# Six output-weight tiles split before the first scores of a latent attention, and four of their product triples left in its tail

## The chip, the cores and the metric

One core of one Trainium2 chip runs the whole program in one launch. The metric is the device time in microseconds (us). TensorE is written PE, VectorE DVE, ScalarE ACT, GpSimd POOL; SP is the engine that issues the DMAs.

## The reference

Four residual blocks over a `(4, 512, 1024)` tensor, each with a layer norm ahead of it. All is float32 at the interface; the kernel carries each matrix operand as a high and a low float16 half and multiplies with three matmuls (high by high, high by low, low by high).

```python
x = x + _L0_attn_ref(_layernorm(x))                 # small attention over the batch axis
x = x + _L0_ffn_ref(_layernorm(x), ...)             # linear + top-2 routed LoRA
x = x + _L1_attn_ref(_layernorm(x), ...)            # 32 heads, causal, 512 tokens x 4 batches
x = x + _L1_ffn_ref(_layernorm(x), ...)             # linear + routed LoRA
# the third one:
q = rmsnorm(x @ wq_a.T) @ wq_b.T ; kv = rmsnorm(ckv) @ wkv_b.T ; rope on q_pe, k_pe
attn = softmax(causal(q_full . k_full * scale))
out = (attn @ v).reshape(B, S, 32 * 128) @ wo.T
```

## The kernel before

The program is a row of blocks, each with five instruction streams (PE, ACT, DVE, POOL, SP) and a barrier of all engines between two blocks: `first` (A), `lora_layer0` (F0), `projections` (C), `attention` (D), `out_projection` (E), `lora_layer1` (F1). An engine works its stream strictly in the written order and waits on semaphores.

**The output weights.** A folds the value half of `wkv_b` into `wo`; the product, 16 tiles of 128x1024 float32 called kt 0 to 15, lies in device memory (`mwd`). Class `OutWeights` takes them in: `sp_load` fetches tile kt into one of three raw buffers (512 KB each; it waits until tile kt - 3 has been split), `act_high` writes its high half (ACT, L479) and `dve_low` its low half (DVE, L483). EARLY = 6 tiles have their halves in `ow_mh`, `ow_ml`, placed before the attention; the other ten live in E. `pe_product(j, kt)` multiplies the attention output of token tile j, transposed by a DMA into `ow_ot`, with tile kt: six matmuls of 512 columns. One product triple is a kt for the token tiles j = 0, 1, 2: 18 matmuls.

**The attention, D.** 128 units u = 0 to 127, one head of one batch for 512 queries each, in a software pipeline that runs u from FIRST = -7 to 134. In round u:
- PE: `scores(u)` (12 matmuls of 512, 384, 256 and 128 columns in three parts, L1657 to L1659, and the causal mask L1666), `values(u-5)` (30 matmuls, L1681 to L1683), `query(u+7)` (6 matmuls of 512), `turn_q(u+2)` (four transposes, L1640); from round 129 on also a product triple.
- ACT: the third part of the exponentials of u-1, `high_p(u-1)` (L1722, the high half of the probabilities), `high_o` (L1741), the first two parts of `exps(u)` (L1714), `nope(u+7)` (L1729), `high_q(u+2)` (L1734), and in the rounds 20, 36, 52, 68, 84, 100 of the table SPLIT one `act_high`.
- DVE: `least` (L1769, the row minima), `bias` (L1778), `rotate(u+6)` (L1799 to L1802), `normalize(u-5)` (L1784, L1788), `low_q(u+2)` (L1807), and in the rounds of SPLIT one `dve_low`.
- POOL: `add_q(u+6)` (L1840), `low_p(u-1)` (L1834), `low_o(u-6)` (L1846).
- SP: `turn_p(u-2)` (L1862, the transpose of the probabilities by DMA, which `values` and, three units on, `high_p` wait for); every 16 rounds `load_w` (L1866, 512 KB of query weights, rounds -6, 10, 26, ... 90); every four rounds `store_o` (L1872, 512 KB of outputs to `od`); three `sp_load` in round 8 (L474), one each in rounds 24, 40, 56, 72, 88, 104; the first pieces of the `ow_ot` transposes (L488, `sp_turn_piece`) in rounds 124, 125, 126, and the second ones in 130 to 132.

Two waits tie the stages: `query(u)` waits for the rotation of unit u-2 (`s_qm`), and part n of the scores waits for the exponentials of part n-4, whose bank it takes:

```python
w.wait_ge(s_qm, u - 1)             # query(u), PE
w.wait_ge(s_exp, n - 3)            # scores, part n, PE
w.wait_ge(s_tl, u + 1)             # scores(u), PE: low_q(u) on DVE is done
w.wait_ge(s_pt[(u - 3) % 4], ...)  # high_p(u), ACT: the transpose of unit u-3 has landed
w.wait_ge(s_ol, u - 1)             # normalize(u), DVE: low_o(u-2) on POOL is done
```

In E the products go on from kt = EARLY, ACT and DVE split the tiles 6 to 15, whose first three raw tiles were loaded in D, and SP fetches the rest and the last `ow_ot` pieces.

Of the kernel before, what the change touches and what calls it, by code (L numbers as in the profile page):

```python
# [17 lines left out]
NT = 16  # L18
# [165 lines left out]
def layers(nc, a, out):  # L184
    root = ExitStack()
    with root:
# [31 lines left out]
        with ExitStack() as right:  # L218
            feed.place(right, "N", "right", 0, (3, 3, 4))
            g["wa"] = SmallWeights(nc, right, a["wa"])  # L220
            lora_layer0(**g)
            g["qT"] = [m("qTh", [128, 2, 2048], H16), m("qTl", [128, 2, 2048], H16)]
# [4 lines left out]
        with ExitStack() as late:  # L227
            ow.raw = [late.enter_context(nc.sbuf_tensor(f"rm{i}", [128, 1024], F, side="right")) for i in range(3)]
            with ExitStack() as outs, ExitStack() as last:
                ow.place(outs)  # L230
                ow.ob = [outs.enter_context(nc.psum_tensor(f"so{i}", [128, 512], F)) for i in range(6)]
                attention(**g)
                mid.close()
                feed.place(last, "N1", "left", 2 * NT, (1, 2, 3))
                lw.place(lambda name, shape, dt=F: last.enter_context(nc.sbuf_tensor(f"F1_{name}", shape, dt)), 1, a,
                         [r[:, 0:784] for r in ow.raw])
                out_projection(**g)
                outs.close()
                lora_layer1(**g)
# [200 lines left out]
class OutWeights:  # L440
# [4 lines left out]

    def __init__(self, nc, root, mwd, od, ms):
# [5 lines left out]

    def place(self, ctx):
# [3 lines left out]
        self.early = [sb(f"m{x}", [128, self.EARLY, 1024]) for x in "hl"]  # L457
# [951 lines left out]
def projections(nc, a, wbs, s_wb, s_xd, cst, half, ident, xb, qT, kT, v, wb0, norm, feed, wa, **_):  # L1409
# [143 lines left out]
    def sp(e):  # L1553
        w = Waits(e)
        e.dma_start(wb0[:, :, :, :], wbs[0]).then_inc(s_wb, 16)
        for t in range(3, NT):
            feed.sp_turn(e, w, NT + t)
        w.wait_ge(s_xd, 16 * NT)
# [10 lines left out]
def attention(nc, wbs, od, s_wb, s_ot, cst, ident, xb, qT, kT, v, wb0, qw, ow, **_):  # L1569
# [35 lines left out]
    SPLIT = [20 + 16 * i for i in range(ow.EARLY)]  # L1605
# [12 lines left out]
    def pe(e):  # L1618
# [67 lines left out]
        for u in range(FIRST, LAST):  # L1686
# [8 lines left out]
            if NU < u <= NU + ow.EARLY:  # L1695
# [7 lines left out]
    def act(e):  # L1703
# [39 lines left out]
        for u in range(FIRST, LAST):  # L1743
            if there(u - 1):
# [11 lines left out]
            if u in SPLIT:  # L1756
                ow.act_high(e, w, SPLIT.index(u))

    def dve(e):
# [49 lines left out]
        for u in range(FIRST, LAST):  # L1809
            if there(u):  # L1810
# [13 lines left out]
            if u in SPLIT:  # L1824
                ow.dve_low(e, w, SPLIT.index(u))
# [30 lines left out]
    def sp(e):  # L1856
# [18 lines left out]
        for u in range(FIRST, LAST):  # L1875
# [6 lines left out]
            if u == SPLIT[0] - 12:  # L1882
                for kt in range(3):
                    ow.sp_load(e, w, kt)
# [512 lines left out]
```

## Time and profile before

| | us |
|---|---|
| median of 3 runs | 1730.37 |
| lowest, highest | 1725.38, 1730.89 |
| the profiled execution | 1732.51 |
| its span | 1730.7 |
| PE busy (share of the span) | 1597.3 (92%) |
| DVE busy | 1029.0 (59%) |
| ACT busy | 873.0 (50%) |
| POOL busy | 816.6 (47%) |
| mean granted TensorE clock | 0.963 |

The profile is of one execution; its own time (1732.51) is its span and 1.8 us around it. Busy shares are means over stages with different limits, so the attention (from about 553 to 1188 us of the span) has to be read by itself. An engine's idle time before an instruction stands in square brackets in the timeline, with what ended it. Matmuls are pipelined: the duration of one overlaps the next, and the distance between two starts is what it costs.

### The profile page before, as it was taken

To read this page: it belongs to the slowest core of one execution; us is meant where nothing else is said; L and a number is where in the kernel's file an instruction comes from. 1 tells how busy PE (TensorE), PEld (TensorE's weight loads), DVE (VectorE), ACT (ScalarE), POOL (GpSimd) and SP (SyncE) were. 2 spreads that over 40 slices of the span, in tenths; PEclk is the share of its full clock that TensorE was granted. 3 is DMA by queue.
4 is the path that set the end of the run, shared out by engine and by line. 5 is a ranking of instruction groups with operands and counts; after the bars stand their busy time and mean duration, and the time that the engine had idled before them with its cause. 6 is when DMAs were issued, how large, how long until landed. Compare 5 with 4: busy or idle time off the path is not lost. (4 is left out here: it accounts for less than half of the span.)

```text
span 1730.7 us, 32183 instructions
## 1 busy us (share of the span) xinstructions
PE 1597.3 (92%) x12482; PEld 980.2 (57%) x12482; DVE 1029.0 (59%) x2766; ACT 873.0 (50%) x1670; POOL 816.6 (47%) x702
## 2 busy tenths in 40 slices
PE   5899579999787999999999999979999999999998
PEld 5566345555443667666767667744444444465554
DVE  5599456776486888888888888852111001154433
ACT  4676322222264899999999999962110000021110
POOL 2222224444474678888888888860010000044440
PEclk7799789999898999999999999989999999999999
DMA  9574333454543599998989999996775413033231
GB/s 320 168 261 173 110 110 86 134 146 122 122 86 62 99 210 172 197 183 169 212 169 194 191 188 187 173 195 173 211 185 113 98 31 79 12 102 86 74 86 74
DMA packets 559608, 249.32 MB, mean 144 GB/s; under 512 B 502240, under 2 KB 535008, under 8 KB 559072
## 3 DMA queue, kind: packets, MB, share of 16 engines
q1 hardware_dynamic: 559456, 247.26, 62.7%
q8 instruction: 99, 1.62, 0.4%
q14 instruction: 53, 0.43, 0.1%
HBM read 73.15 MB, written 48.23 MB: 70 GB/s over the span
## 5 line engine op out<-in xcount | busy, mean ns | idle before, releaser
L1834 POOL TENSOR_TENSOR xb<-xb 128x1280 f16<-128x1280 f32 x128 | 335.4, 2620 | 7.6 <-ACT xb L1722 7.6
L1714 ACT ACTIVATE xb<-so,D_sv,qw_c 128x512 f32<-128x512 f32 (+3 forms) x512 | 288.7, 621 | 8.2 <-DVE D_sv L1778 8.1
L1769 DVE TENSOR_REDUCE so<-so 128x1 f32<-128x512 f32 (+3 forms) x512 | 227.7, 491 | 7.8 <-PE so L1666 7.3
L1722 ACT ACTIVATE xb<-xb 128x1280 f16<-128x1280 f32 x128 | 162.6, 1271 | 15.2 <-DMA xb<-xb 11.3
L1657 PE MATMUL so<-kTh,D_QTh 128*128 128x512 f16 (+3 forms) x512 | 153.6, 300 | 15.8 <-ACT xb L1714 15.8
L92 POOL TENSOR_SCALAR mv<-mv 128x1 f32<-128x1 f32 x64 | 27.6, 431 | 285.9 <-DVE mv L87 284.8
L1958 DVE SCALAR_TENSOR_TENSOR xb<-so,ms_c,xb 128x512 f32<-128x512 f32 x32 | 22.5, 746 | 228.2 <-PE so L50 228.2
L1658 PE MATMUL so<-kTl,D_QTh 128*128 128x512 f16 (+3 forms) x512 | 153.2, 299 | 0.0
L1659 PE MATMUL so<-kTh,D_QTl 128*128 128x512 f16 (+3 forms) x512 | 146.6, 299 | 0.0
L168 POOL TENSOR_TENSOR N_hl<-N_h,N_hl 128x1024 f16<-128x1024 f32 x48 | 103.6, 2158 | 88.3 <-ACT N_hl L163 88.2
L1840 POOL TENSOR_TENSOR D_qs<-D_qs,D_t 128x256 f32<-128x256 f32 x128 | 92.9, 726 | 90.6 <-DVE D_t L1802 90.6
L1681 PE MATMUL D_t<-vh,xb 128*128 128x65 f16 x1280 | 132.2, 195 | 3.3 <-DVE D_on L1788 3.3
L1682 PE MATMUL D_t<-vl,xb 128*128 128x65 f16 x1280 | 132.3, 193 | 0.0
L1683 PE MATMUL D_t<-vh,xb 128*128 128x65 f16 x1280 | 131.7, 194 | 0.0
L1807 DVE TENSOR_TENSOR D_QTl<-D_t,D_QTh 128x512 f16<-128x512 f32 x128 | 88.6, 692 | 63.8 <-ACT D_QTh L1734 63.8
L48 PE MATMUL so<-E_mh,ow_ot 128*128 128x512 f16 x320 | 121.9, 381 | 2.9 <-DVE E_ml L483 2.9
L50 PE MATMUL so<-E_mh,ow_ot 128*128 128x512 f16 x320 | 122.0, 381 | 0.0
L49 PE MATMUL so<-E_ml,ow_ot 128*128 128x512 f16 x320 | 121.9, 381 | 0.0
L1681 PEld LDWEIGHTS D_t<-vh,xb 128*128 128x128 f16 x1280 | 119.6, 98 | 3.8 <-issue 1.7
L1682 PEld LDWEIGHTS D_t<-vl,xb 128*128 128x128 f16 x1280 | 119.3, 99 | 0.4
L1683 PEld LDWEIGHTS D_t<-vh,xb 128*128 128x128 f16 x1280 | 119.5, 97 | 0.0
L163 ACT ACTIVATE N_hl<-N_h 128x1024 f16<-128x1024 f32 x48 | 50.4, 1050 | 112.0 <-DVE N_h L105 111.6
(248 smaller groups left out, 4245.6 us busy)
## 6 DMA issues: line engine op xcount, KB each, us to landing
A_wo<-in_wo SPq DMA_DIRECT2D x16, 1024.0 KB, 6.1
od<-D_os SPq DMA_DIRECT2D x32, 512.0 KB, 4.4
mwd<-A_mst SPq DMA_DIRECT2D x32, 256.0 KB, 2.4
xd<-xb SPq DMA_DIRECT2D x16, 512.0 KB, 4.1
rm<-mwd SPq DMA_DIRECT2D x16, 512.0 KB, 5.0
xb<-xd SPq DMA_DIRECT2D x16, 512.0 KB, 5.8
out_x<-xb SPq DMA_DIRECT2D x16, 512.0 KB, 3.3
xb<-in_x SPq DMA_DIRECT2D x6, 1024.0 KB, 19.7
```

The source lines that it names most:

```text
L48: e.matmul(out, a[0], b[0], start=start, stop=False, **kw)
L50: return e.matmul(out, a[1], b[0], start=False, stop=stop, **kw)
L1657: e.matmul(ps, qh, kT[0][:, k0:k0 + M], start=i > 0, stop=False)
L1658: e.matmul(ps, qh, kT[1][:, k0:k0 + M], start=False, stop=False)
L1659: e.matmul(ps, ql, kT[0][:, k0:k0 + M], start=False, stop=False)
L1681: e.matmul(o, pt[:, c, :], v[0][:, t, 0:65], start=j == 0, stop=False)
L1682: e.matmul(o, pt[:, c, :], v[1][:, t, 0:65], start=False, stop=False)
L1683: m = e.matmul(o, pt[:, 10 + c, :], v[0][:, t, 0:65], start=False, stop=j == i)
L1714: m = e.activation(p[:, AT[i]:AT[i] + N], Sb[n % 4][:, c:c + N], ACT.Exp, scale=qw.col(qw.NEG, g), bias=s[:, 7 - i:8 - i])
L1722: e.activation(P2[u % 3][:, 0:1280], P[u % 3][:, :], ACT.Copy).then_inc(s_ph, 1)
L1769: m = e.tensor_reduce(minima(u, i), Sb[n % 4][:, c:c + N], AX.X, ALU.min)
L1834: e.tensor_tensor(P2[u % 3][:, 1280:2560], P[u % 3][:, :], P2[u % 3][:, 0:1280], ALU.subtract).then_inc(s_pl, 1)
```

## The change

The six tiles are no longer split in the rounds 20 to 100 but in the rounds -7 (kt 0, 1, 2), -2 (kt 3) and -1 (kt 4, 5), at the head of the round on ACT and DVE. Their raw buffers and halves are placed ahead of the projections, whose SP stream loads tiles 0 to 2 at its end; tiles 3 to 5 are loaded in round -7, tiles 6 to 8 together in round 64. PE does the triples of kt 0 to 3 in D (rounds 129 to 132) and those of kt 4 and 5 at the head of E. The first `ow_ot` pieces are issued in rounds 123 to 125. The raw buffers are named `ow_raw` now.

```diff
     EARLY = 6
+    AHEAD = 4
+    def place_weights(self, ctx):
+        def sb(name, shape, dt):
+            return ctx.enter_context(self.nc.sbuf_tensor(f"ow_{name}", shape, dt))
+        self.raw = [sb(f"raw{i}", [128, 1024], F) for i in range(3)]
+        self.early = [sb(f"m{x}", [128, self.EARLY, 1024], H16) for x in "hl"]
...
 # projections, sp
         for t in range(3, NT):
             feed.sp_turn(e, w, NT + t)
+        for kt in range(3):
+            ow.sp_load(e, w, kt)
         w.wait_ge(s_xd, 16 * NT)
...
 # attention
-    SPLIT = [20 + 16 * i for i in range(ow.EARLY)]
+    SPLIT = [FIRST, FIRST, FIRST, -2, -1, -1]
...
 # pe
-            if NU < u <= NU + ow.EARLY:
+            if NU < u <= NU + ow.AHEAD:
...
 # act (and dve with ow.dve_low)
         for u in range(FIRST, LAST):
+            for kt in range(ow.EARLY):
+                if SPLIT[kt] == u:
+                    ow.act_high(e, w, kt)
...
-            if u in SPLIT:
-                ow.act_high(e, w, SPLIT.index(u))
...
 # sp
-            if u == SPLIT[0] - 12:
-                for kt in range(3):
+            if u == FIRST:
+                for kt in range(3, ow.EARLY):
                     ow.sp_load(e, w, kt)
-            if u - 4 in SPLIT:
-                ow.sp_load(e, w, SPLIT.index(u - 4) + 3)
-            if u == NU - 4:
+            if u == NU // 2:
+                for kt in range(ow.EARLY, ow.EARLY + 3):
+                    ow.sp_load(e, w, kt)
+            if u == NU - 5:
                 w.wait_ge(s_ot[0], 16 * 15)
-            if NU - 4 <= u < NU - 4 + ow.G:
-                ow.sp_turn_piece(e, u - NU + 4, 0)
+            if NU - 5 <= u < NU - 5 + ow.G:
+                ow.sp_turn_piece(e, u - NU + 5, 0)
...
 # out_projection, pe
-        for kt in range(EARLY, 12):
+        for kt in range(ow.AHEAD, 12):
```

The start of D on DVE, as the change has it (L1808 to L1811 is a rotation, L1816 a `low_q`, L1778 the first minima; before, they were L1799 to L1802, L1807 and L1769):

```order
L489 SCALAR_TENSOR_TENSOR ow_ml<-ow_raw,ms_c,ow_mh 128x1024 x3
L1808 TENSOR_TENSOR D_qs<-so,cst 128x4x64
L1810 TENSOR_TENSOR D_t<-so,cst 128x4x32
L1811 TENSOR_TENSOR D_t<-so,cst 128x4x32
...
L489 SCALAR_TENSOR_TENSOR ow_ml<-ow_raw,ms_c,ow_mh 128x1024
L1808 TENSOR_TENSOR D_qs<-so,cst 128x4x64
L1810 TENSOR_TENSOR D_t<-so,cst 128x4x32
L1811 TENSOR_TENSOR D_t<-so,cst 128x4x32
L1816 TENSOR_TENSOR D_QTl<-D_t,D_QTh 128x512
L489 SCALAR_TENSOR_TENSOR ow_ml<-ow_raw,ms_c,ow_mh 128x1024 x2
```

Three low halves stand ahead of the first rotation, one ahead of the fifth, and two between the first and the second `low_q`; before there was none here. ACT has its six `act_high` in the same rounds.

The end of D on SP, before (L1862 is `turn_p`, L488 a piece of `ow_ot`, L1872 a store):

```order
L1862 DMA_TRANSPOSE xb<-xb 128x20x128 x2
L488 DMA_TRANSPOSE ow_ot<-od 128x8x128
L1862 DMA_TRANSPOSE xb<-xb 128x20x128
L488 DMA_TRANSPOSE ow_ot<-od 128x8x128
L1862 DMA_TRANSPOSE xb<-xb 128x20x128
L1872 DMA od<-D_os 128x4x512
L488 DMA_TRANSPOSE ow_ot<-od 128x8x128
L1862 DMA_TRANSPOSE xb<-xb 128x20x128 x3
```

and now (L1872 is `turn_p`, L494 a piece, L1882 a store):

```order
L1872 DMA_TRANSPOSE xb<-xb 128x20x128
L494 DMA_TRANSPOSE ow_ot<-od 128x8x128
L1872 DMA_TRANSPOSE xb<-xb 128x20x128
L494 DMA_TRANSPOSE ow_ot<-od 128x8x128
L1872 DMA_TRANSPOSE xb<-xb 128x20x128
L494 DMA_TRANSPOSE ow_ot<-od 128x8x128
L1872 DMA_TRANSPOSE xb<-xb 128x20x128
L1882 DMA od<-D_os 128x4x512
L1872 DMA_TRANSPOSE xb<-xb 128x20x128 x3
```

Each of the three pieces now goes out one `turn_p` earlier: they stand ahead of the transposes of units 122, 123 and 124.

## Rows read from the trace of the kernel before

**Rows 1.** Windows of the attention's middle: busy us (count) of PE, PEld, DVE, ACT, POOL, clock, DMA share, GB/s
```profile
625.00:1126.00 501.00, 492.67 (x6105) 352.13 (x6104) 436.12 (x1309) 484.73 (x877) 433.84 (x327) 1.00 0.99 185
```

**Rows 2.** Timeline of PE and ACT, one unit apart: start us, us, engine, line, tiles
```profile
755.93 0.38 PE L1657 MATMUL so<-kTh,D_QTh 128*128 128x512 f16 x1
760.43 0.38 PE L1657 MATMUL so<-kTh,D_QTh 128*128 128x512 f16 x1
...
758.30 1.27 ACT L1722 ACTIVATE xb<-xb 128x1280 f16<-128x1280 f32 x1
762.71 1.27 ACT L1722 ACTIVATE xb<-xb 128x1280 f16<-128x1280 f32 x1
```

**Rows 3.** Waits from 625 to 1126 us: total us, times, longest
```profile
PE so L1657 <- ACT xb L1714: 8.3, 8, 1.4
ACT xb L1722 <- DMA xb<-xb: 7.1, 7, 2.3
```

**Rows 4.** Timeline of the first split unit, on ACT, DVE and PE
```profile
662.59 1.16 ACT L479 ACTIVATE ow_mh<-rm,ms_c 128x1024 f16<-128x1024 f32 x1
663.78 1.99 DVE L483 SCALAR_TENSOR_TENSOR ow_ml<-rm,ms_c,ow_mh 128x1024 f16<-128x1024 f32 x1 [0.35 <-ACT ow_mh L479]
666.65 0.38 PE L1659 MATMUL so<-kTh,D_QTl 128*128 128x512 f16 x1
667.97 0.34 PE L1657 MATMUL so<-kTh,D_QTh 128*128 128x384 f16 x1 [0.94 <-ACT xb L1714]
```

**Rows 5.** Waits of ACT for a transpose of the probabilities, and PE after the first
```profile
617.86 1.27 ACT L1722 ACTIVATE xb<-xb 128x1280 f16<-128x1280 f32 x1 [3.15 <-DMA xb<-xb]
703.46 1.27 ACT L1722 ACTIVATE xb<-xb 128x1280 f16<-128x1280 f32 x1 [1.93 <-DMA xb<-xb]
778.21 1.27 ACT L1722 ACTIVATE xb<-xb 128x1280 f16<-128x1280 f32 x1 [2.32 <-DMA xb<-xb]
...
620.15 0.34 PE L1657 MATMUL so<-kTh,D_QTh 128*128 128x384 f16 x1 [1.96 <-ACT xb L1714]
```

**Rows 6.** Windows after the stalls at 620, 1160 and 1188 us, columns as in rows 1
```profile
620.00:625.00 5.00, 4.85 (x48) 3.46 (x49) 3.48 (x11) 4.97 (x10) 3.17 (x4) 0.66 0.93 256
1160.00:1165.00 5.00, 5.00 (x16) 1.85 (x15) 0.00 (x0) 0.00 (x0) 0.15 (x1) 0.61 1.18 232
1188.00:1195.00 7.00, 4.17 (x12) 1.64 (x13) 3.68 (x3) 3.23 (x3) 0.00 (x0) 0.76 0.86 133
```

**Rows 7.** Line 483 by form: ns min/median/max, first and last start
```profile
L483 DVE SCALAR_TENSOR_TENSOR E_ml<-rm,ms_c,E_mh x10: 1277/1284/1286, 1189.4 to 1211.8; 128x1024 f16<-128x1024 f32 x10
L483 DVE SCALAR_TENSOR_TENSOR ow_ml<-rm,ms_c,ow_mh x6: 1840/1853/1987, 663.8 to 1033.6; 128x1024 f16<-128x1024 f32 x6
```

**Rows 8.** Timeline of the start of the attention, on PE, DVE and ACT
```profile
553.00 0.58 PE L48 MATMUL so<-wb,qTh 128*128 128x512 f16 x1 [1.69 <-PEq L1560]
...
556.17 0.42 DVE L1799 TENSOR_TENSOR D_qs<-so,cst 128x256 f32<-128x256 f32 x1 [3.49 <-ACT D_qs L1729]
567.39 1.16 DVE L1769 TENSOR_REDUCE so<-so 128x1 f32<-128x512 f32 x2 [0.42 <-PE so L1666]
...
568.85 1.34 ACT L1714 ACTIVATE xb<-so,D_sv,qw_c 128x512 f32<-128x512 f32 x2 [2.60 <-DVE D_sv L1778]
```

**Rows 9.** Timeline of the end of the attention, on SP, DVE and PE
```profile
1148.83 3.63 SPq L1862 DMA_TRANSPOSE xb<-xb  x1
...
1153.13 1.50 SPq L488 DMA_TRANSPOSE ow_ot<-od  x1
...
1153.90 0.42 DVE L1788 TENSOR_TENSOR D_on<-D_t,D_sv 128x256 f32<-128x256 f32 x1 [0.81 <-POOL D_os L1846]
...
1159.66 0.58 PE L48 MATMUL so<-ow_mh,ow_ot 128*128 128x512 f16 x1 [3.38 <-DMA ow_ot<-od]
```

**Rows 10.** PE on the two sides of the barrier between attention and output projection
```profile
1187.57 0.38 PE L50 MATMUL so<-ow_mh,ow_ot 128*128 128x512 f16 x1
1190.83 0.38 PE L48 MATMUL so<-E_mh,ow_ot 128*128 128x512 f16 x1 [2.89 <-DVE E_ml L483]
```

More of the change, by code:

```diff
@@ L221, in layers @@
             lora_layer0(**g)
+            ow.place_weights(root)
             g["qT"] = [m("qTh", [128, 2, 2048], H16), m("qTl", [128, 2, 2048], H16)]
@@ L226, in layers @@
             projections(**g)
[L227 to L239, printed above, removed]
+        with ExitStack() as outs, ExitStack() as last:
+            ow.place(outs)
+            ow.ob = [outs.enter_context(nc.psum_tensor(f"so{i}", [128, 512], F)) for i in range(6)]
+            attention(**g)
+            mid.close()
+            feed.place(last, "N1", "left", 2 * NT, (1, 2, 3))
+            lw.place(lambda name, shape, dt=F: last.enter_context(nc.sbuf_tensor(f"F1_{name}", shape, dt)), 1, a,
+                     [r[:, 0:784] for r in ow.raw])
+            out_projection(**g)
+            outs.close()
+            lora_layer1(**g)
 class Scope:
@@ L456, in place @@
         self.OT = [sb(f"ot{i}", [128, 8, 2, 2, 128]) for i in range(self.G)]
-        self.early = [sb(f"m{x}", [128, self.EARLY, 1024]) for x in "hl"]
     def pe_product(self, e, w, j, kt):
@@ L1406, in lora_layer0, with projections @@
     ph.ctx.close()
-def projections(nc, a, wbs, s_wb, s_xd, cst, half, ident, xb, qT, kT, v, wb0, norm, feed, wa, **_):
+def projections(nc, a, wbs, s_wb, s_xd, cst, half, ident, xb, qT, kT, v, wb0, norm, feed, wa, ow, **_):
     ph = Scope(nc, "C")
@@ L1809, in dve @@
         for u in range(FIRST, LAST):
+            for kt in range(ow.EARLY):
+                if SPLIT[kt] == u:
+                    ow.dve_low(e, w, kt)
             if there(u):
@@ L1823, in dve @@
                 low_q(u + 2)
-            if u in SPLIT:
-                ow.dve_low(e, w, SPLIT.index(u))
     def pool(e):
```

## The prediction

> **What bounds the kernel now.** First the windows of the attention's middle [rows 1]: PE is busy 492.67 of 501 us at full clock and ACT 484.73, so both are nearly full, and a busy share alone does not say which one sets the pace. So next two consecutive units [rows 2]: PE starts its scores 4.50 us apart (755.93 to 760.43) with no idle time noted, ACT starts `high_p` 4.41 us apart (758.30 to 762.71). ACT's round is the shorter by 0.09 us: PE sets the pace as long as nothing interrupts, and ACT wins back 0.09 us a unit after an interruption, until it has caught up. The cost of an interruption is therefore what it leaves on PE. The waits of that stretch [rows 3] say how often: PE waited for ACT's exponentials 8 times, 8.3 us. Six of the eight are the units with a split, two lie right behind ACT's longest waits for a transpose of the probabilities. The two places behind the middle where PE stands are the first product triple and the barrier [rows 9, 10]. The last stages, from 1195 us on, are PE at full work, and nothing there changes but when they start.
>
> By 0.3% either way I mean 5.2 us of the 1730.37, about what a measurement of this kernel can tell from no change. I sum against the profiled execution's own 1732.5 us, which is 2.1 us above the median of the runs.
>
> **1. The six splits leave the middle: -6.6 us.** In the first one [rows 4] ACT works 1.16 us on the high half and DVE 1.99 on the low one, starting one after the other; `high_p` then comes 2 us late over two units, and of this 1.10 us reach PE: the next part of the scores starts 1.32 us after the one before instead of 0.22. So about 0.9 us of slack is there ahead of an interruption and the rest is PE's. The five later ones repeat it within 0.01 us. 6 x 1.10 = 6.6. What covered them is PE's own round, and that is what remains: 4.50 us a unit. Bounds: 0.94 each as the idle time noted (5.6) to 1.16 each, all of ACT's piece (7.0).
>
> **2. Loads against transposes: -1.1 us.** The transposes of the probabilities take the DMA queue nearly all the time (DMA share 0.99, rows 1). The three loads of round 8 went out in one go ahead of one; ACT waited 3.15 us, PE 1.96 by the idle time noted, 2.12 by starts [rows 5], and then ran from 620 to 625 us at a granted clock of 0.66, which is 1.2 GHz for two thirds of it: 5 x 0.34 = 1.7 us more [rows 6]. The single loads of rounds 24 and 40 came two rounds before a `load_w`, and ACT waited 1.93 and 2.32 us [rows 5]; behind it PE lost 8.3 - 6 x 0.94 = 2.7 us by the waits [rows 3], 3.0 by starts. In all 2.1 + 1.7 + 3.0 = 6.8. After the change no tile is loaded in these rounds, but `load_w` stays with its store beside it, and from this trace I can't separate the two. I leave 1.0 us at round 10 and 0.5 each at 26 and 42, two fifths of the old ones. The three loads now meet at round 64. The nearest row is that of round 8: ACT waits 3.15, the full slack of 0.9 is there, PE loses 2.2, and the clock may fall as it did, 1.7 more. That is 5.9 against 6.8, so -1 us. Bounds: nothing at all is left (-6.8), or everything stays and the loads of round 64 come on top with a fall of the clock (+3.9).
>
> The Trainium skill, "DMA: Bandwidth & Descriptors", section Queues, rings and completion order, says that each DMA engine consumes its descriptors in ring order, and this speaks against bundling loads on the queue of the transposes: what is issued first is in the way whatever it is for. The row at 617.86 us agrees.
>
> **3. The six splits at the start: +4.7 us.** This is the price. The new duration of a low half is bounded by two rows [rows 7]: 1.28 us in the output projection, where POOL is idle, 1.85 in the attention's middle, where POOL works all the time. In rounds -7 to -1 POOL has only the short additions, so I take 1.28. By the Trainium skill, "SBUF — State Buffer", section Who interferes with whom, a DVE instruction with two SBUF inputs contends with a POOL instruction that reads SBUF; it would put these six at the uncontended duration too. No run here shows them at this place yet.
> Step by step from 553.0 [rows 8]: ACT starts the three high halves at once (their raw tiles were loaded about 10 us earlier), DVE starts its first at 554.2 and ends the third at 554.2 + 3 x 1.28 = 558.0. The first rotation starts there instead of at 556.17, +1.8. Queries go in pairs behind rotations (`query(u)` waits for the rotation of u-2), so PE stands about 1.4 us ahead of `query(2)` and runs 1.2 us late until `query(5)` ends at 564.2. The fourth high half waits behind `nope(4)` and ends at 564.4; its low half puts the fifth rotation and the first `low_q` to 565.7 and 566.5. Two low halves (2.6 us) then stand before the sixth rotation and the second `low_q`, which ends at 571.0. The first minima follow, at 571.0 instead of 567.39, and the first exponentials at 572.5 instead of 568.85: +3.65. From there the first units go at ACT's pace, as before, so all of it arrives. To this I add 1.0 for the clock: PE now stands still three times for 1.4 to 2 us, and a stand of 2.1 us was followed by a fall [rows 5, 6]. Bounds: 3.0, if the raw tiles' waits and the pairs overlap better; 3.65 + 6 x 0.57 = 7.1 with the low halves at 1.85, and 8 with two falls of the clock. The loads at the end of the projections stand behind all transposes of that stage, and the tiles 3 to 5 in round -7 are ahead of nothing but a `load_w` that is needed 16 units later: 0.
>
> **4. The first piece transposes go one unit earlier: -3.0 us.** PE waited 3.38 us for the third piece before the first triple (to 1159.66) [rows 9]. Issued ahead of the transpose of unit 124 instead of behind it, the piece goes out some 4.4 us earlier (1153.13 to about 1148.7) and lands before PE asks. But each piece takes the SP queue 1.3 to 1.5 us in front of a transpose that `high_p` waits for: the last units slip by 1.4 at the most, `values(124)` with them (its turn hangs on `normalize`, which hangs on POOL, which hangs on `high_p`). So the triple starts at about 1156.7 in the old times. Bounds: 0 to 3.6. PE is at half clock there in both (0.61 from 1160 to 1165 us) [rows 6], so no more comes of it.
>
> **5. Two triples cross the barrier: -4.2 us.** Each is 18 matmuls of 512 columns at some 0.22 us from start to start [rows 4], 3.9 us, in both kernels: moved, not saved. But E began with a wait: PE's last start in D is 1187.57, its first in E 1190.83 [rows 10], since the raw tile 6 could only be split by ACT (1.15) and DVE (1.28) behind the barrier. Now 7.8 us of products with halves that are long ready stand there, and the splits of tiles 6, 7 and 8 run beside them. Of the 3.26 us about 0.75 remain for the barrier itself (between C and D, ACT, DVE and PE are at work 0.3 us after the last engine's end), -2.5. The clock fell behind this wait as well: 7 x 0.24 = 1.7 us [rows 6], which goes with it. Bounds: -1.5 to -4.3. The new pieces of `ow_ot` that E asks for at kt 8 were in time by less than a microsecond; now PE comes to kt 8 3.9 us later after the barrier, so they are late nowhere.
>
> **Sum.** -6.6 - 1.1 + 4.7 - 3.0 - 4.2 = -10.2 us: 1722.3 of the profiled 1732.5. Against the median that is **1720**.
>
> **Rivals.**
> *The start and the loads eat more.* The low halves take 1.85 us at the start, or the clock falls twice (+8 instead of +4.7), and the `load_w` stalls stay as they are (+1 instead of -1.1). For it: the start is a chain with no slack (DVE idles there only behind ACT and PE). Against it: POOL idles. -10.2 + 3.3 + 2.1 = -4.8: 1725.5.
> *The loads hide.* The pair of a load and a `load_w` did harm, not either alone: the single load of round 104, which had no `load_w` behind it, made nobody wait, and of the 7 waits counted [rows 3] six came behind a pair and one, 0.7 us, behind the single load of round 24. And the pairs of rounds 72 and 88 cost PE nothing. Then the old 6.8 go and round 64 costs little, with the start at 3.7: -10.2 - 4.7 - 1.0 = -16: 1714.5.
> *The DMA becomes the bound (slower).* The transposes fill the queue (0.99), and the PE gaps of the splits were time in which they caught up. If the queue and not PE's 4.50 us holds the middle, the six gaps come back as waits of ACT for transposes, the pieces at the end gain nothing (they only push transposes), and round 64 adds 2.7. It decides when a transpose lands later than `high_p` three units on can bear, some 2.9 us beyond what an undisturbed one takes. Then +2.7 + 4.7 - 4.2 = +3.2: 1733.6. Against it: between the loads ACT never waits for a transpose [rows 3], even in stretches of 16 units.
> *The change doesn't do what it says.* The order of the instructions shows the splits where they are meant to be; only part 4 could be without effect, and 0 is in its bounds.
>
> **How the numbers follow.** 1720 with its own range of 1717 to 1724: 0.57. The start eats more, around 1725.5: 0.19. The loads hide, around 1714.5: 0.17. The DMA bound, around 1733.6: 0.07. The range 1714 to 1726 takes in the first, more than half of the second and most of the third. Faster by over 0.3% is below 1725.2: all of the first and third and a third of the second, 0.80. Within 0.3%: the rest of the second and most of the fourth, 0.17. Slower: 0.03.
>
> **What would show it.** In the middle no idle time of PE at rounds 20 to 100, and 4.50 us a unit throughout; the wait of ACT for a transpose near round 66, about 3 us, and smaller ones after rounds 10, 26, 42. The first minima 3.5 to 5 us later after the barrier than now (14.4 us), and low halves of 1.28 us. The first triple without a wait for `ow_ot`, and the first E matmul within 1 us of D's last at clock 1.00. The prediction is wrong if the start costs over 8 us, or if PE's gaps come back in the middle with ACT waiting for transposes.

## The result, and the profile after

Over six runs each the changed kernel takes 1712.78 us (1711.59 to 1715.57), the one before 1727.49 (1725.38 to 1730.89; the three runs known at the prediction lay high, their median was 1730.37). The ratio is 0.9914 with a 95% interval of 0.99 to 0.9929, so the change takes off 14.7 us (12.3 to 17.3), where 10.2 were forecast. The sign was right. The time lies 1.2 us below the range's low end, 1714.

| | before, us | after, us | |
|---|---|---|---|
| the profiled execution, its span | 1732.5, 1730.7 | 1713.0, 1711.2 | -19.5 in the span |
| `first` (A), same code | 188.6 | 183.2 | -5.4 |
| layer 0's second block, projections, layer 1's second block | 585.9 | 586.8 | +0.9 |
| D: first query to the first `high_p` | 18.79 | 22.26 | +3.5 |
| D: from there to `low_q(120)` | 542.90 | 531.13 | -11.8 |
| D: from there to the first triple | 44.98 | 44.51 | -0.5 |
| D: from there to the last `values` | 16.43 | 16.02 | -0.4 |
| last `values` to F1's first matmul | 333.09 | 327.29 | -5.8 |

From D's first query to F1 that is -15.0, which agrees with the times. The 5.4 us of `first` are no effect of the change: its code is the same, and over all seventeen profiles of this study it lasts 180.9 to 188.6 us, in the kernels with the old attention as in those with the new. The two executions profiled lay nearly at the two ends. Every comparison below is therefore made inside D and E, or by medians of many runs on one chip.

Windows of the profile after; columns as in rows 1:

```profile
625.00:1108.00 483.00, 480.95 (x5984) 345.79 (x5983) 421.00 (x1280) 472.67 (x854) 420.17 (x320) 1.00 0.98 185
870.00:875.00 5.00, 3.37 (x49) 2.40 (x50) 2.04 (x5) 4.97 (x10) 3.25 (x2) 1.00 1.13 261
1146.00:1151.00 5.00, 5.00 (x25) 2.16 (x23) 0.61 (x2) 1.07 (x4) 4.46 (x4) 0.63 1.09 216
1166.00:1173.00 7.00, 6.55 (x32) 2.80 (x30) 3.67 (x3) 3.23 (x3) 0.00 (x0) 1.00 0.77 173
1356.00:1366.00 10.00, 10.00 (x54) 6.17 (x53) 1.96 (x5) 2.57 (x3) 1.01 (x1) 0.83 0.51 107
```

The same two stretches of the kernel before (the last one lies 20 us later there):

```profile
625.00:1108.00 483.00, 474.67 (x5879) 338.90 (x5878) 420.24 (x1261) 466.85 (x845) 418.12 (x315) 1.00 0.99 186
1376.00:1386.00 10.00, 10.00 (x46) 5.98 (x45) 1.97 (x5) 2.62 (x3) 1.01 (x1) 0.66 0.50 107
```

In the middle PE stands still for 2.05 us of 483 and no longer for 8.3. Nearly all of what is left is one place. Waits of the middle after, from 590 to 1108 us (total us, times, longest):

```profile
ACT xb L1730 <- DMA xb<-xb: 7.1, 5, 3.0
PE so L1665 <- ACT xb L1722: 2.1, 2, 1.8
```

The same for the kernel before, from 590 to 1126 us:

```profile
ACT xb L1722 <- DMA xb<-xb: 10.3, 8, 3.1
PE so L1657 <- ACT xb L1714: 10.3, 9, 2.0
```

ACT still waits five times for a transpose, 7.1 us in all, but PE notices only two of the five. The longest is the one that the three loads of round 64 cause, in the timeline of SP, ACT and PE:

```profile
857.57 1.60 SPq L480 DMA_DIRECT2D ow_raw<-mwd  x3
859.27 10.35 SPq L1872 DMA_TRANSPOSE xb<-xb  x2
...
869.33 1.27 ACT L1730 ACTIVATE xb<-xb 128x1280 f16<-128x1280 f32 x1 [2.97 <-DMA xb<-xb]
...
871.63 0.34 PE L1665 MATMUL so<-kTh,D_QTh 128*128 128x384 f16 x1 [1.80 <-ACT xb L1722]
```

It is the stall of round 8 over again ([rows 5]: 3.15 and 1.96), moved to round 64. In this profile the clock did not fall behind it: 1.00 from 870 to 875 us, against 0.66 in [rows 6]. In another profile of the same kernel (changed_fourth, below) it did, and as far as before:

```profile
875.00:880.00 5.00, 4.89 (x49) 3.69 (x50) 3.40 (x10) 4.97 (x10) 2.93 (x3) 0.66 1.10 246
```

Where `act_high` used to stand, nothing interrupts PE, and the single `load_w` of rounds 10, 26, 42 leave it 0.42 us in all, all of it behind round 26. (Over the twelve profiles with a `load_w` alone in round 26 and no split in the middle, this place costs 0 to 0.83 us.)

The start of D, on ACT, DVE and PE:

```profile
548.46 3.23 ACT L485 ACTIVATE ow_mh<-ow_raw,ms_c 128x1024 f16<-128x1024 f32 x3 [1.02 <-PEq L1568]
549.63 3.68 DVE L489 SCALAR_TENSOR_TENSOR ow_ml<-ow_raw,ms_c,ow_mh 128x1024 f16<-128x1024 f32 x3 [1.48 <-ACT ow_mh L485]
553.23 0.42 DVE L1808 TENSOR_TENSOR D_qs<-so,cst 128x256 f32<-128x256 f32 x1
...
562.54 2.57 DVE L489 SCALAR_TENSOR_TENSOR ow_ml<-ow_raw,ms_c,ow_mh 128x1024 f16<-128x1024 f32 x2
...
566.36 1.15 DVE L1778 TENSOR_REDUCE so<-so 128x1 f32<-128x512 f32 x2
...
562.17 0.38 PE L48 MATMUL so<-wb,qTh 128*128 128x512 f16 x1 [1.92 <-DVE D_t L1811]
```

D's first query is at 548.48 here (553.00 in [rows 8]). The first low half starts 1.15 us behind it, the first minima 17.9 us behind it, where they used to be 14.4 behind. The low halves, by the view of line 489 (ns min/median/max):

```profile
L489 DVE SCALAR_TENSOR_TENSOR ow_ml<-ow_raw,ms_c,ow_mh x6: 1272/1284/1378, 549.6 to 563.8; 128x1024 f16<-128x1024 f32 x6
```

They take 1.28 us and not the 1.85 of the middle [rows 7], with POOL nearly idle. The Trainium skill, "SBUF — State Buffer", section Who interferes with whom, says that a DVE instruction with two SBUF inputs contends with a POOL instruction that reads SBUF; the trace agrees. PE stood still twice, for 1.06 and 1.92 us, and the clock was 1.00 behind both.

The end of D, on SP and PE:

```profile
1125.82 1.30 SPq L494 DMA_TRANSPOSE ow_ot<-od  x1
1127.20 3.67 SPq L1872 DMA_TRANSPOSE xb<-xb  x1
1130.92 1.90 SPq L494 DMA_TRANSPOSE ow_ot<-od  x1
1132.91 3.32 SPq L1872 DMA_TRANSPOSE xb<-xb  x1
1136.28 1.30 SPq L494 DMA_TRANSPOSE ow_ot<-od  x1
1137.68 3.51 SPq L1872 DMA_TRANSPOSE xb<-xb  x1
...
1136.50 0.34 PE L1665 MATMUL so<-kTh,D_QTh 128*128 128x384 f16 x1 [1.61 <-ACT xb L1722]
1144.73 0.24 PE L1689 MATMUL D_t<-vh,xb 128*128 128x65 f16 x1 [3.13 <-DMA xb<-xb]
...
1146.37 0.62 PE L48 MATMUL so<-ow_mh,ow_ot 128*128 128x512 f16 x1
```

The first triple no longer waits for its piece (3.38 us in [rows 9]). In its place the products with V wait 3.13 us for a transpose of the probabilities, which stands behind the pieces on SP. In this pair of profiles the wait changed its name and hardly its size; the other profiles, below, show that this is not the rule.

The barrier, on PE; the last matmul of D and the first of E:

```profile
1166.09 0.38 PE L50 MATMUL so<-ow_mh,ow_ot 128*128 128x512 f16 x1
1166.92 0.38 PE L48 MATMUL so<-ow_mh,ow_ot 128*128 128x512 f16 x1 [0.45 <-PEq L1906]
```

0.83 us from start to start, against 3.26 in [rows 10], and the clock stays at 1.00 behind it (0.76 in [rows 6]).

### The profile page after: what moved, and what is told of

Read it like the earlier page. It is cut to its first block and busy times, and to the rows that moved or that the text cites. A ratio compares the mean times of both kernels' runs of the same rounds, so it can differ in the third digit from the quotient of the medians.

```text
span 1711.2 us, 32182 instructions
## 1 busy us (share of the span) xinstructions
PE 1585.0 (93%) x12482; PEld 974.3 (57%) x12482; DVE 1028.6 (60%) x2766; ACT 875.8 (51%) x1670; POOL 810.7 (47%) x702
## 5 line engine op out<-in xcount | busy, mean ns | idle before, releaser
L1778 DVE TENSOR_REDUCE so<-so 128x1 f32<-128x512 f32 (+3 forms) x512 | 228.1, 492 | 19.3 <-PE so L1674 18.6
L1816 DVE TENSOR_TENSOR D_QTl<-D_t,D_QTh 128x512 f16<-128x512 f32 x128 | 88.5, 692 | 48.7 <-ACT D_QTh L1742 48.7
```

The source lines that it names most:

```text
L1778: m = e.tensor_reduce(minima(u, i), Sb[n % 4][:, c:c + N], AX.X, ALU.min)
```

## Experiments

Ratios are to the kernel before, run on the same chip in turn with the experiment, with their 95% interval. "Middle" is the fifth row of the table above; the kernel before has 542.90 us there, the changed one 531.13. "Gap" is a distance between two PE starts, less what it is in an undisturbed unit.

### Only part 5, and only part 4

**ahead_only** is the kernel before, with two triples taken across the barrier:

```diff
-            if NU < u <= NU + ow.EARLY:
+            if NU < u <= NU + 4:
...
-        for kt in range(EARLY, 12):
+        for kt in range(4, 12):
```

> The kernel before with only part 5 of the change: PE does the triples of kt 0 to 3 in the attention's tail and those of kt 4 and 5 at the head of the output projection. The prediction's theory: -4.2 us, the wait of 3.3 us at the barrier down to 0.75 and the fall of the clock behind it gone. What the changed kernel's trace suggests: up to -5.8, since the stretch behind the last values became 5.8 us shorter there; if that surplus of 1.6 is not of the barrier but of where the clock falls at the small column sums in the output projection, this kernel shows it or not by chance, and the gap at the barrier alone gives 4 to 4.3. A rival, that the splits in the middle hold the time and the tail is covered: 0.

Measured: 0.9973 (0.9959 to 0.9987) of 1725.3 us, that is -4.7 us (-7.1 to -2.2). From the last `values` to F1 its trace takes 327.30 us, just as the changed kernel, instead of 333.09. PE across the barrier:

```profile
1178.37 0.38 PE L48 MATMUL so<-ow_mh,ow_ot 128*128 128x512 f16 x1 [0.45 <-PEq L1895]
```

Of the 5.8 us, 2.4 are the gap at the barrier (3.05 to 0.61), 1.7 the slow clock behind it, and 1.7 a term that the sum did not have: 190 us later PE does sums over single columns, and the clock falls behind them, to 0.66 over ten microseconds before, to 0.83 here as in the changed kernel (windows above), 10 x 0.17 = 1.7 us less. Whether an edit does this is open; it comes up again below. Nor is the slow clock behind the old barrier there every time: loads_moved and pieces_only (both below) have the same start-to-start distance of 3.27 us at it, and the clock falls behind it in loads_moved and stays at 1.00 in pieces_only. The gap is the sure part of the gain.

**pieces_only** is the kernel before with its pieces issued one unit earlier (`NU - 4` made `NU - 5` in its three places).

> The kernel before with only part 4: the first three pieces of ow_ot go out in rounds 123 to 125 instead of 124 to 126. The prediction's theory: -3.0 us (0 to -3.6), since PE waited 3.4 us for the third piece. The rival, from the changed kernel's trace: the pieces push the transposes of units 122 to 124 by 1.3 us each and these add up, so that values(124) comes about as late as the third piece did: -0.5 us, with no wait for ow_ot but longer waits of ACT for transposes (over 1 us three times) before it.

Measured: 0.9989 (0.9973 to 1.0004), -1.9 us (-4.7 to +0.7): no difference that is sure. From `low_q(120)` to the last `values` its trace takes 58.1 us, against 61.4 before. The first triple comes 1.8 us earlier (43.2 us behind `low_q(120)` for 45.0), and between it and the last `values` the slow clock took 0.6 us here and 2.1 there.

### The pieces back, in the changed kernel

**pieces_back** undoes part 4 alone:

```diff
-            if u == NU - 5:
+            if u == NU - 4:
                 w.wait_ge(s_ot[0], 16 * 15)
-            if NU - 5 <= u < NU - 5 + ow.G:
-                ow.sp_turn_piece(e, u - NU + 5, 0)
+            if NU - 4 <= u < NU - 4 + ow.G:
+                ow.sp_turn_piece(e, u - NU + 4, 0)
```

> The changed kernel with its pieces back in rounds 124 to 126. The prediction's theory: 3.0 us slower than the changed kernel. The rival, that the earlier pieces pay for themselves with pushed transposes: within 1 us of it, with the wait for the third piece (3 us) back before the first triple and the waits of ACT for transposes gone.

Measured: 0.9942 (0.9922 to 0.9962), with the changed kernel not on the same chip. So both were run side by side twice more.

> The changed kernel once more, beside the next one on one chip: about 14 us below before. In its trace the time from the 121st low half of the queries to the first triple is 43 to 44.5 us, as in the two profiles of it so far.

> The changed kernel with its pieces back in rounds 124 to 126, beside the changed kernel on the same chip, since the two were compared over different chips. The prediction's theory: 3.0 us slower. What the profiles so far suggest (44.7 us to the first triple against 43.1 to 44.5): no more than 1.5 us slower, as pushed transposes pay for the earlier pieces.

The changed kernel took 1712.13 us, the one with the pieces back 1715.02: 2.9 us. Once more on another chip:

> The changed kernel, beside the next one on one chip, for the price of the earlier pieces: 0.991 of the time before, as three times already.

> The changed kernel with its pieces back in rounds 124 to 126. So far 0.9942 and 0.9936 of the time before against 0.9914, 0.9911 and 0.9910 of the changed kernel, some 4 us, while the profiles showed no difference from the last units to the output projection (387.3 to 387.9 us here, 384.9 to 387.8 there). The prediction's theory: 3.0 us slower once more, so that the profiles were the slower executions of the changed kernel. The rival: under 1 us.

1713.81 and 1714.84: 1.0 us, with ratios whose intervals overlap (0.9908 to 0.9939, and 0.9918 to 0.9947), as they do in the first pair (0.9884 to 0.9937, and 0.9913 to 0.9958). With pieces_only this makes three comparisons by whole runs, all with the earlier pieces ahead, by 1.0 to 2.9 us; these runs settle the price of part 4 no closer.

The traces scatter as much. Counted from `low_q(120)`, those of the first pair reach the first triple after 44.2 us (changed) and 43.6 (pieces back), and the last `values` after 60.4 and 60.1; those of the second pair after 43.5 and 44.9, and after 58.6 and 62.1. One pair shows no gain, the other 1.4 and 3.5 us. Over the fifteen profiles with the pieces in these rounds, the six with rounds 124 to 126 reach the first triple after 43.6 to 45.5 us (mean 44.6) and the last `values` after 60.1 to 62.7 (61.2); the nine with 123 to 125 after 42.7 to 44.7 (43.7) and 57.6 to 61.2 (59.2). By the means the edit gains 0.9 and 2.0 us, with ranges that overlap.

Two things stand against each other there. The wait for a piece before the first triple, 0.9 to 4.1 us in the six, is gone in all nine. But a piece ahead of the transposes of units 122, 123 and 124 makes `high_p` of the following units late (in the first pair those of units 124 to 127 come 24.0, 29.3, 32.9 and 39.1 us behind the scores of unit 120, with the pieces back 23.2, 27.3, 31.0 and 37.5), and the `values` behind them. The wait of the `values` for a transpose, 3.13 us in the profile above, is not of the edit alone: waits of 1.9 to 3.1 us stand there in four of the nine and in three of the six.

### The loads, taken apart

**loads_spread** is the changed kernel with tiles 6, 7 and 8 loaded one at a time, far from any `load_w`:

```diff
-            if u == NU // 2:
-                for kt in range(ow.EARLY, ow.EARLY + 3):
-                    ow.sp_load(e, w, kt)
+            if u in (52, 68, 84):
+                ow.sp_load(e, w, ow.EARLY + (u - 52) // 16)
```

> The changed kernel with the three loads of round 64 apart, one each in rounds 52, 68 and 84, six rounds ahead of a load of query weights. If three loads in one go are what costs (ACT waits 3 us, PE loses 2.0 in the changed kernel's trace): -2 us against the changed kernel, no wait of ACT over 1 us between 840 and 900 us. If any load of 512 KB costs PE its share wherever it stands: no change, three smaller stalls.

Measured: 0.9898 (0.988 to 0.9915), -17.6 us. The middle takes 528.93 us and its one gap is 0.35 us. Its window and waits, as for the changed kernel (the waits from 590 to 1105 us):

```profile
625.00:1108.00 483.00, 482.82 (x6020) 347.76 (x6018) 424.18 (x1286) 476.54 (x857) 421.86 (x322) 1.00 0.98 186
```

```profile
ACT xb L1730 <- DMA xb<-xb: 3.2, 4, 1.4
PE so L1665 <- ACT xb L1722: 0.2, 1, 0.2
```

So the burst of round 64 costs 2 us (1.75 to 2.12 in its seven profiles), and a tile load by itself nothing. That a pair would have cost more does not follow from this run: its loads also stand late, where the pairs of the kernel before cost PE nothing either. loads_moved and loads_paired ask about that.

**loads_moved** asks the same of the kernel before: all six splits stay in the middle, and only the loads of tiles 0 to 5 and 6 to 8 move away from round 8 and from the `load_w`.

```diff
-            if u == SPLIT[0] - 12:
+            if u == FIRST:
                 for kt in range(3):
                     ow.sp_load(e, w, kt)
-            if u - 4 in SPLIT:
-                ow.sp_load(e, w, SPLIT.index(u - 4) + 3)
+            if u - 13 in SPLIT:
+                ow.sp_load(e, w, SPLIT.index(u - 13) + 3)
```

> The kernel before with its splits where they were, but its tile loads away from the loads of query weights: three in round -7, one each in rounds 33, 49, 65, 81, 97, 113, seven rounds behind a load of query weights. If it is the pair that does harm (a tile load two rounds ahead of a load of query weights with its store): PE's gaps behind waits for transposes (1.8, 1.5, 1.3 us in three profiles) shrink to under 0.5 each and the kernel is 4 to 5 us faster than before. If the load of query weights does it by itself, as the prediction assumed for two fifths of it: only the 1.8 us of round 8 go and 0.5 each of the others, -2 to -3 us.

Measured: 0.9969 (0.9951 to 0.9987), -5.3 us (-8.4 to -2.2), without a split or a triple touched. Its waits from 590 to 1115 us:

```profile
ACT xb L1722 <- DMA xb<-xb: 5.5, 6, 1.8
PE so L1657 <- ACT xb L1714: 6.4, 7, 0.9
```

PE's gaps are the six of the splits, 1.10 us each as before, and one of 0.91, behind the `load_w` of round 42, which now stands by itself. In the kernel before they were 2.12 behind the three loads of round 8, 1.61 behind the pair of rounds 24 and 26, and 1.42 behind that of rounds 40 and 42. The tile loads of rounds 33 and 49, nearly as early and alone, cost nothing. The middle is 537.45 us, against 542.90.

**loads_paired** is the changed kernel with tiles 6, 7 and 8 loaded where the old kernel had its singles, two rounds ahead of a `load_w` (`if u in (24, 40, 56)` in loads_spread).

> The changed kernel with its three loads of round 64 apart, one each in rounds 24, 40, 56, two rounds ahead of a load of query weights, as the tile loads stood in the kernel before. The run with rounds 52, 68, 84 lost 0.4 us of PE in the whole middle. If the pair does the harm by itself: ACT waits some 2 us for a transpose at two or three of these places and PE loses 0.5 to 1.5 us behind each, 2 to 4 us in all over that run. If it took the splits of the middle to make the pairs hurt (they used up ACT's slack): PE loses under 1 us.

Measured: 0.9917 (0.9892 to 0.9942), -14.3 us. The middle takes 530.65 us, with gaps of 0.92 and 1.07 behind the first two pairs and none behind the third; waits from 590 to 1105 us:

```profile
ACT xb L1730 <- DMA xb<-xb: 5.5, 4, 2.1
PE so L1665 <- ACT xb L1722: 1.7, 2, 0.9
```

What a place costs PE, over all profiles (us; n is their number):

| | `load_w` alone | with a tile load two rounds ahead |
|---|---|---|
| round 26, no split in the middle | 0 to 0.83, n = 12 | 0.92, n = 1 |
| round 42, no split in the middle | 0, n = 12 | 1.07, n = 1 |
| round 26, splits in the middle | 0, n = 1 | 1.43 to 1.61, n = 3 |
| round 42, splits in the middle | 0.91, n = 1 | 1.25 to 1.42, n = 3 |
| rounds 58, 74, 90, with or without splits | 0 | 0, once 0.46 |

A tile load alone costs nothing anywhere. The pair costs more than the `load_w` alone at rounds 26 and 42, with the splits and without them, by 0.1 to 1.6 us; at the later rounds it costs next to nothing. The runs don't show why the place matters. In times, loads_paired (0.9892 to 0.9942) and loads_spread (0.988 to 0.9915) are not surely apart.

### Other places for the splits

The changed kernel was run again beside these.

> The changed kernel itself, as the reference for the other three of this call on the same chip: 0.9914 of the time before (0.990 to 0.993) was measured. Every theory gives that again. Its stage times in the trace say how much of a difference between two profiles is chance: the small attention of layer 0 (the first 180 us) differed by 5 us between the two profiles though its code is the same.

0.9911 (0.9884 to 0.9939), 1709.59 us where the kernel before took 1723.6.

**three_in_tail** splits tiles 3 to 5 in D's last rounds, where ACT and DVE have little to do, and loads 6 to 8 behind the last piece instead of in round 64:

```diff
-    SPLIT = [FIRST, FIRST, FIRST, -2, -1, -1]
+    SPLIT = [FIRST, FIRST, FIRST, 129, 130, 131]
...
-            if u == NU // 2:
-                for kt in range(ow.EARLY, ow.EARLY + 3):
-                    ow.sp_load(e, w, kt)
...
                 ow.sp_turn_piece(e, u - NU - 2, 1)
+                if u == NU + 4:
+                    for kt in range(ow.EARLY, ow.EARLY + 3):
+                        ow.sp_load(e, w, kt)
```

> The changed kernel with the splits of tiles 3, 4, 5 in rounds 129 to 131, where ACT and DVE stand idle, and tiles 6 to 8 loaded in round 132 instead of together in round 64. If the start costs by its chain of DVE work: three of six low halves go, the first exponentials come 2.0 to 2.5 us earlier (19 to 20.3 us to the first high half of the probabilities instead of 22.3), and the 2 us that PE loses at round 64 go too: -4 us against the changed kernel. If the start's price is the wait for the first split (ACT, then DVE) and not the number of splits: only the 2 us of round 64. Should the tiles 6 to 8 arrive late, PE waits at the third triple of the output projection.

Measured: 0.9893 (0.9866 to 0.9919), 1707.52 us, 2.1 below the changed kernel, where 4 were expected. The start is 20.01 us instead of 22.27, and the middle 528.73 instead of 530.40. The tail takes some of this back in the trace: 61.2 us from `low_q(120)` to the last `values`, the longest of the nine profiles with the pieces in rounds 123 to 125, with the clock at half for 13.7 us. Whether the splits of the last rounds do this is open. And the middle shows what it is without any tile's load or split:

```profile
600.00:1100.00 500.00, 500.00 (x6217) 360.02 (x6216) 439.60 (x1333) 493.52 (x890) 436.69 (x334) 1.00 0.97 183
```

PE is busy for 500 of 500 us, with the transposes at a DMA share of 0.97. From the scores of unit 6 to those of unit 120 it takes 513.6 us, and 114 units of 4.50 are 513: the middle is PE's, and there is nothing left in it to win but PE's own work.

**splits_in_C** is loads_spread with all six splits in the projections, at every second token tile from 4 to 14, and their loads between the feeds there:

```diff
+    AT_T = [4, 6, 8, 10, 12, 14]
...
+            if t in AT_T:
+                ow.act_high(e, w, AT_T.index(t))
...
+            if t in AT_T:
+                ow.dve_low(e, w, AT_T.index(t))
```

> The kernel with one load each in rounds 52, 68, 84, and all six splits inside the projections, one every second tile on ACT and DVE, where ACT waits 2 us in each tile for POOL; nothing is split in the attention. If that stage is held by its chain over POOL and the slack of ACT and DVE takes the splits: the projections stay at 93 us, the attention's start goes back to 18.8 us, and the kernel is 5.5 us faster than the changed one. If the splits delay the chain: up to 1.2 us each, 7 us in the projections, and the gain is gone.

Measured: 0.991 (0.9884 to 0.9935), 1709.82 us. D starts 3.3 us faster (19.00 us), and the projections take 96.5 us instead of 93.6 (92.3 to 94.9 in all other profiles): what the start of D paid is paid there. Beside loads_spread nothing is won.

### The pieces where their data is ready

**pieces_mid** takes the six piece transposes of `ow_ot` out of the tail. The first three read what the units up to 19 have stored, the other three what those up to 51 have, so they can go out in the middle of D:

```diff
-            if u == NU - 5:
-                w.wait_ge(s_ot[0], 16 * 15)
-            if NU - 5 <= u < NU - 5 + ow.G:
-                ow.sp_turn_piece(e, u - NU + 5, 0)
-            if NU + 2 <= u < NU + 2 + ow.G:
-                ow.sp_turn_piece(e, u - NU - 2, 1)
+            if u in (48, 64, 80):
+                w.wait_ge(s_ot[0], 16 * 3)
+                ow.sp_turn_piece(e, (u - 48) // 16, 0)
+            if u in (96, 104, 112):
+                w.wait_ge(s_ot[0], 16 * 7)
+                ow.sp_turn_piece(e, (u - 96) // 8, 1)
```

and the three loads of round 64 stand in round 68.

> The changed kernel with all six early pieces taken out of the attention's last rounds: the pieces of kt 0 to 3 in rounds 48, 64, 80, those of kt 4 to 7 in rounds 96, 104, 112 (the head groups that they transpose are stored by rounds 26 and 58), and the tile loads of round 64 in round 68. If it is pieces against transposes on the SP queue that holds the tail: ACT's waits for transposes in the last five units shrink from 1 to 1.5 us each to under 0.5, the first triple comes without a wait, 3 to 5 us less from the last units to the first triple, and the middle loses under 1 us. If the last values hang on DVE, ACT and POOL alone: 1 us or less.

Measured: 0.9876 (0.985 to 0.9902), 1706.79 us, where the changed kernel took 1712.13 on the same chip: -5.3, for the pieces and the moved loads together. SP in the tail:

```profile
1121.89 14.90 SPq L1872 DMA_TRANSPOSE xb<-xb  x4
1136.84 0.57 SPq L1882 DMA_DIRECT2D od<-D_os  x1
1137.51 7.66 SPq L1872 DMA_TRANSPOSE xb<-xb  x2
```

From `low_q(120)` to the first triple it is 41.28 us, where the changed kernel had 44.19 and the one with the pieces back 43.62. The middle did not get longer for its six additional transposes (529.46 us); with the loads in round 68 instead of 64 even the gap of 2 us behind them is gone, in this one profile: ACT waits 0.99 us there and PE not at all. So 1.5 us of the gain are of the middle by the traces. Why four rounds matter there was not tried on its own.

**combined** is three_in_tail with these pieces.

> The kernel with the splits of tiles 3 to 5 in rounds 129 to 131 and no load in round 64, and with the early pieces in rounds 48 to 112 as in the run before this one. If both effects stand side by side: 3 us below the changed kernel from the first and 3 to 5 from the second, some 20 us below before. If the tail has one bound that neither moves: no better than the first alone.

Measured: 0.9868 (0.9843 to 0.9893), 1704.16 us: 22.6 us below the kernel before and 8.0 below the changed one. It has the lowest time of all; of the 2.6 us below pieces_mid, 2.25 are the shorter start (20.01 us instead of 22.26). Against three_in_tail only the pieces differ: the first triple comes after 41.40 us instead of 44.70, and the middle with its six more transposes takes 528.86 us instead of 528.73. From D's first query to F1 that is 3.4 us less (933.87 for 937.22), the price of the pieces' place by itself. PE still waits before its first triple, but for the units' own chain:

```profile
1138.13 0.21 PE L1689 MATMUL D_t<-vh,xb 128*128 128x65 f16 x1 [1.50 <-DVE D_on L1797]
```

## Why the prediction was right and where it was not

| term | forecast, us | in the traces, us | by whole runs |
|---|---|---|---|
| 1. six splits leave the middle | -6.6 | -6.6 | |
| 2. loads against transposes | -1.1 | -5.2 | -5.3 for moving the loads alone |
| 3. splits at the start | +4.7 | +3.5 | |
| 4. pieces one unit earlier | -3.0 | -0.9 | -1.9, -2.9, -1.0 |
| 5. two triples across the barrier | -4.2 | -5.8 | -4.7 for this alone |
| sum | -10.2 | -15.0 | -14.7 |

**Part 1 held.** loads_moved, with the splits in place and the loads elsewhere, keeps six gaps of 1.10; three_in_tail, with neither, has none at all.

**Part 2 is the step that failed.** The old cost was read well: 6.8 us forecast; the middle before minus that of three_in_tail and minus the splits is 542.9 - 528.7 - 6.6 = 7.6. What failed is the sentence "I leave 1.0 us at round 10 and 0.5 each at 26 and 42, two fifths of the old ones", and with it the "1.7 more" for a fall of the clock behind round 64. Measured in the first profile are 0.42 at all `load_w` together, 1.96 at round 64, and no fall of the clock: 2.4 and not 5.9. (The prediction's own figures, 5.9 against 6.8, make this part -0.9; its heading and its sum have -1.1. Nothing hangs on the 0.2.)

The first error is the share. A stall was divided between the transfers around it, two fifths for the `load_w`, as if their costs stood side by side. They don't: in loads_paired the transpose issued with the `load_w` of round 42 lands 14.2 us behind the end of its unit's `high_p`, in two profiles of the changed kernel, with the `load_w` alone, 12.6 and 12.9 behind it. ACT waits 2.11 us in the one and 0.5 to 0.8 in the others, and PE, with some 0.9 us of slack ahead of it, loses 1.07 and nothing. The row of round 104, a load alone which nobody waited for, said so, and only the rival used it. The second error is the fall of the clock at its full 1.7: it came in one of the seven profiles with the loads of round 64 (changed_fourth).

That rival, *the loads hide*, came nearest with 1714.5, and its reason ("the pair of a load and a `load_w` did harm, not either alone") is in the main what loads_moved and loads_paired show, at rounds 26 and 42. It erred in letting round 64 cost little: the triple load leaves 2 us there. The rival in which the start and the loads eat more fell on both counts (+3.5 and -5.2 us).

**Part 3.** The chain was right: low halves at 1.28 us, first minima 3.5 us later for 3.6 forecast. The 1.0 us for the clock did not come. PE stood still twice, not three times, for up to 1.92 us, and lost none of its clock.

**Part 4** took the wait of 3.38 us for the piece as the thing to win and the transposes' slip as a side effect of 1.4 at the most. Both are of one queue, and the slips add up: `high_p(126)` comes 36.3 to 36.6 us behind `low_q(120)` in the nine profiles with the earlier pieces, 34.4 to 35.3 in the six with the later ones. "So the triple starts at about 1156.7 in the old times", 3.0 earlier, became 0.5 earlier between the profiles of before and after, and 0.9 by the means of the fifteen; by whole runs the edit is worth 1.0 to 2.9 us. pieces_mid and combined show that more was to be had, and how: with the pieces out of the queue's critical stretch the first triple comes after 41.3 and 41.4 us, earlier than in any of the other fifteen.

**Part 5.** Gap and clock behind the barrier went as forecast (-2.4 and -1.7, forecast -2.5 and -1.7), though in pieces_only the clock did not fall behind the same gap: that half of the term is not there in every execution. The further 1.7 us stand at the column sums, 190 us later, and are no part of what was forecast.

**The rival on the slow side**, the DMA as the bound of the middle, fell: with a DMA share of 0.97 PE is busy 500 of 500 us.

**The base.** The three runs of before that were known lay 2.9 us above the median of six. From 1727.5 the same working gives 1717.3 with a range of 1711 to 1723, which holds 1712.8. That would be a hit by luck: the traces have part 2 off by 4.1, part 3 by 1.2 and part 5 by 1.6 to the fast side, and part 4 by 2.1 to the slow one. These make 4.8 together, with the 2.9 of the base 7.7, where the forecast and the time are 7.2 apart; the traces' -15.0 for -14.7 by medians, and rounding, are the difference.

## What to carry to other kernels

When small transfers share a queue with transposes that a chain waits for, don't give each of them a share of a stall. A tile load alone was free here; two transfers within two rounds cost about 1 us and more at two early places and next to nothing at three later ones; three at once cost 2 us at rounds 8 and 64 and nothing at 68. Such a price has to be taken from the place itself, and trying another place is a change of one line: moving the loads alone took 5.3 us off (loads_moved), against 3.1 net by the traces for moving the six splits to a start that has no slack. A transfer that waits in a critical tail although its data has been stored for over seventy rounds belongs where the queue has room; put one place forward in the same stretch, it won 1 to 3 us and pushed the transposes behind it. Before costing a move by a difference of two traces, look at a stage that the change doesn't touch: here one varied by 7.7 us from one execution to the next.

## What was not expected of the hardware

- *The clock behind a short stand of PE.* Ten profiles have a stand of PE behind three tile loads in one go, in round 8 or 64. In two of them it was 2.12 us, and both times the clock fell and 1.7 us were lost (0.66 over five microseconds [rows 6], and the window of changed_fourth above). In the other eight it was 1.75 to 1.96 us, and nothing was lost. Two cases don't show whether the length of the stand decides it. The window behind the stand of 1.81 us in pieces_only:

```profile
614.00:619.00 5.00, 4.00 (x54) 2.95 (x55) 2.67 (x8) 4.97 (x10) 3.25 (x2) 1.00 1.04 251
```

  A single fall in a single trace was no ground to charge another one in full. In the tail of D, between `low_q(120)` and the last `values`, the clock takes 1.7 to 6.8 us, in steps of 1.7, and differs between profiles of one kernel; part of the scatter of part 4 is this.
- *Sums over single columns.* Behind 28 matmuls of one column (3.2 to 3.7 us) in the output projection the clock falls in some executions, and the loss comes in steps of 1.7 us: clock 0.66 over ten microseconds in the kernel before and in loads_moved (3.4 us), 0.83 in most of the changed ones (1.7), 1.00 in pieces_only, loads_spread and loads_paired (none). The window of pieces_only, beside the two shown above:

```profile
1363.00:1373.00 10.00, 10.00 (x62) 6.32 (x61) 1.96 (x5) 2.62 (x3) 1.02 (x1) 1.00 0.58 107
```

  The steps do not follow the edits (the changed kernel itself has 0.83 in three profiles and none in the fourth), and what sets them stays open. The two profiles with two steps are those in which the clock had also fallen behind the barrier. One step is about the size of part 4, so a difference of two traces that runs across this place says little.
- *`first` varies by 7.7 us* over the executions (180.9 to 188.6) with one and the same code; its cause was not looked for.
